# The first cross-attention of a Perceiver block: another order of key copies, scores, output projection and weighing

## The reference, cut to what matters

```python
def _L0_xattn_ref(query, key, value, mask, Wq, bq, Wk, bk, Wv, bv, Wo, bo):   # 16 heads of 16
    q = _split_heads(query @ Wq + bq)
    k = _split_heads(key @ Wk + bk)
    v = _split_heads(value @ Wv + bv)
    scores = jnp.einsum('bhqd,bhkd->bhqk', q, k) / jnp.sqrt(jnp.asarray(HS, q.dtype))
    scores = scores + mask * -1000000000.0
    attn = jax.nn.softmax(scores, axis=-1)
    out = jnp.einsum('bhqk,bhkd->bhqd', attn, v)
    out = out.transpose(0, 2, 1, 3).reshape(query.shape[0], query.shape[1], -1)
    return out @ Wo + bo
x = x + _L0_xattn_ref(_layernorm(x, axis=-1), ctx_1024, ctx_1024, mask, ...)
x = x + _L0_attn_ref(...)       # self-attention with compressed keys
x = x + _L0_ffn_ref(...)        # 8 experts, top 2
x = x + _L1_xattn_ref(...)      # the second cross-attention
x = x + _L1_attn_ref(...)
x = x + _L1_ffn_ref(...)
```

## Time and profile before

| what | value |
|---|---|
| median of 3 runs | 1205.26 us (1203.36 to 1205.91) |
| the profiled execution, its own time | 1215.15 us |
| its span in the trace | 1213.3 us |
| TensorE matmuls busy over the span | 946.6 us (78%) |
| VectorE busy | 581.1 us (48%) |
| ScalarE busy | 454.8 us (37%) |
| GpSimd busy | 338.9 us (28%) |
| first cross-attention, first scores to last addition to x | 26.2 to 252.0 us of the span |

### The profile page before, as it was taken

How to read it: one execution, slowest core, us unless ns; L and a number is a source line. 1 busy time by engine, 2 the same in 40 slices (tenths; PEclk the granted TensorE clock), 3 DMA queues, 4 the chain that set the end, 5 groups by cost and what they waited for, 6 DMA issues and landing times.

```text
span 1213.3 us, 24253 instructions
## 1 busy us (share of the span) xinstructions
PE 946.6 (78%) x8634; PEld 747.8 (62%) x8634; DVE 581.1 (48%) x1758; ACT 454.8 (37%) x1306; POOL 338.9 (28%) x502
## 2 busy tenths in 40 slices
PE   5899999979786399999814788888887663399980
PEld 3677777744664199999703556656555553399980
DVE  4556556530564201111276688788886563022222
ACT  3566666633222033333202465555555551011000
POOL 3211112001100500000262577666863241300004
PEclk9899999989797599999957799999998885699995
DMA  8111116000000678888310011111000001689953
GB/s 259 37 37 37 36 35 235 2 1 0 1 1 1 234 300 321 330 332 326 121 39 35 1 37 36 37 37 35 0 2 1 2 2 55 244 305 333 336 190 104
DMA packets 50562, 135.76 MB, mean 112 GB/s; under 512 B 16168, under 2 KB 37552, under 8 KB 44464
## 3 DMA queue, kind: packets, MB, share of 16 engines
q1 hardware_dynamic: 47408, 126.28, 29.1%
q0 software_dynamic: 3072, 8.39, 2.1%
HBM read 117.35 MB, written 17.30 MB: 111 GB/s over the span
## 4 chain that ended last, share of the span: by engine, by line
PE 59%; DVE 22%; issue 8%; POOL 3%; ACT 2%; SPq 2%; DMA 1%; another core or an unknown queue 1%; DVEq 0%; POOLq 0%; ACTq 0%
PE lower L998 14%; PE upper L1007 10%; PE upper L619 7%; PE upper L587 5%; PE upper L655 3%; PE lower L641 2%; PE upper L672 2%; PE upper L780 2%; PE upper L689 2%; DVE arena L1417 2%; DVE arena L1389 1%; DVE arena L1453 1%; POOL xslot L1941 1%; PE upper L957 1%; DVE x L1785 1%
## 5 line engine op out<-in xcount | busy, mean ns | idle before, releaser
L998 PEld LDWEIGHTS lower<-arena 128*128 128x128 f32 x1472 | 175.1, 195 | 6.1 <-DVE arena L1751 3.9
L998 PE MATMUL lower<-arena 128*128 128x128 f32 x1472 | 176.0, 279 | 2.6 <-DVE arena L1751 2.6
L619 PE MATMUL upper<-wkv,arena 128*128 128x256 f32 x512 | 141.3, 400 | 12.0 <-ACT arena L1098 6.8
L1007 PE MATMUL upper<-arena 128*128 128x256 f32 x552 | 126.4, 379 | 0.0
L1947 POOL DMA_INDIRECT arena<-yslot,slot x32 | 30.8, 962 | 323.4 <-DMA yslot<-arena 314.3
L619 PEld LDWEIGHTS upper<-wkv,arena 128*128 128x128 f32 x512 | 91.0, 193 | 34.8 <-issue 12.4
L1007 PEld LDWEIGHTS upper<-arena 128*128 128x128 f32 x552 | 101.5, 190 | 12.0
L1312 ACT ACTIVATE arena<-lower,arena 128x128 f32<-128x128 f32 x184 | 52.4, 370 | 106.4 <-PE lower L998 106.4
L1123 ACT ACTIVATE arena<-lower,arena 128x257 f32<-128x257 f32 x128 | 59.6, 475 | 61.0 <-DVE arena L1395 61.0
L1851 POOL TENSOR_TENSOR arena<-arena 128x512 f32<-128x512 f32 x64 | 70.6, 1114 | 36.1 <-ACT klast L1176 20.7
L655 PE MATMUL upper<-const,arena 128*128 128x128 f32 x512 | 78.0, 275 | 1.7 <-ACT arena L1133 1.4
(11 more groups left out here) (231 smaller groups left out, 1727.6 us busy)
## 6 DMA issues: line engine op xcount, KB each, us to landing
arena<-in_ew_dram SPq DMA_DIRECT2D x23, 2048.0 KB, 7.1
arena<-in_ew_dram SPq DMA_DIRECT2D x23, 1536.0 KB, 6.1
arena<-in_ctxT_dram SPq DMA_DIRECT2D x16, 1028.0 KB, 5.2
xslot<-zero SPq DMA_DIRECT2D x2, 2944.0 KB, 15.2
arena<-xslot SPq DMA_DIRECT2D x46, 128.0 KB, 5.8
yslot<-arena SPq DMA_DIRECT2D x46, 128.0 KB, 6.1
const<-in_const_dram SPq DMA_DIRECT2D x1, 1151.0 KB, 7.6
x<-in_x_dram SPq DMA_DIRECT2D x1, 1024.0 KB, 5.7
```

What stands on the lines that cost most here:

```text
L619: ins = mm(bank[6 + w][:, 0:D], dctx[k2][:, c, j2, w * P:w * P + P], wkv[l][:, c, D:2 * D], start=(c == 0), stop=(c == KC - 1))
L998: ins = mm(bank[1 + half][:, i * P:i * P + P], ew[k][:, at:at + P], exT[k % 2][:, c, :], start=(c == 0), stop=(c == KC - 1))
L1007: ins = mm(bank[4 + k % 2][:, 0:D], eh[k % 2][:, i, :], ew[k][:, at:at + D], start=(i == 0), stop=(i == nh - 1))
```

## The change

It gives the first cross-attention (`l` = 0) slot orders of its own on TensorE, ScalarE and VectorE. The second keeps the order it had. No instruction is added or taken away, and no function that a slot calls is changed.

- TensorE: scores, turns 0, keys 0, keys 1, values 0, project, turns 1, values 1, weigh.
- ScalarE: turned, keys 0, keys 1, exps 0, exps 1, values 0, values 1, shared.
- VectorE: maxima, shares, merge of batch b - 1, added, turned.
- GpSimd and SyncE are unchanged.

```diff
@@ TensorE
+                def first_slot(n, k, j, it):
+                    scores(n, k, j, it)
+                    turns(n, k, j, it, 0)
+                    keys(n, k, j, it, 0)
+                    keys(n, k, j, it, 1)
+                    values(n, k, j, it, 0)
+                    if there(n):
+                        project(n, k, j)
+                    turns(n, k, j, it, 1)
+                    values(n, k, j, it, 1)
+                    weigh(n, k, j, it)
+
                 def slot(n, k, j, it):
+                    if l == 0:
+                        first_slot(n, k, j, it)
+                        return
                     turns(n, k, j, it, 0)
                     scores(n, k, j, it)
@@ ScalarE
+                def first_slot(n, k, j, it):
+                    turned(n, k, j, it)
+                    keys(n, k, j, it, 0)
+                    keys(n, k, j, it, 1)
+                    exps(n, k, j, it, 0)
+                    exps(n, k, j, it, 1)
+                    values(n, k, j, it, 0)
+                    values(n, k, j, it, 1)
+                    shared(n, k, j, it)
+
                 def slot(n, k, j, it):
+                    if l == 0:
+                        first_slot(n, k, j, it)
+                        return
                     turned(n, k, j, it)
                     squares(n, k, j, it)
@@ VectorE
+                def first_slot(n, k, j, it):
+                    n0, k0, j0, _ = ahead(n, k, j, it, -1)
+                    maxima(n, k, j, it)
+                    shares(n, k, j, it)
+                    if there(n0):
+                        merge(n0, k0, j0)
+                    if j == 1 and there(n) and not (isinstance(n, int) and n == 0):
+                        added(n - 1)
+                    turned(n, k, j, it)
+
                 def slot(n, k, j, it):
+                    if l == 0:
+                        first_slot(n, k, j, it)
+                        return
                     n0, k0, j0, _ = ahead(n, k, j, it, -1)
                     if there(n0):
                         merge(n0, k0, j0)
```

## The result

The changed kernel takes 1214.45 us, the median of four runs (1208.82 to 1215.74; a fifth execution on record took 1218.91), against 1205.39 for the kernel before in the same comparison: 9.1 us slower. The ratio on record is 1.0079, with a 95% interval of 1.0041 to 1.0116. A second comparison gave 1.0068 (1.0042 to 1.0093). Both the forecast direction and the stated range (1200 to 1216) hold. The point (1209.6) lies 4.9 us low, and the median lies just outside what the prediction called its forecast's own range, 1205 to 1214.

The account below looks back on a forecast made before the run. TensorE's stream was taken to set the pace in the first cross-attention. Terms -1.1 + 0.7 + 6.6 - 0.6 - 1.3 = +4.3 us on 1205.26 gave 1209.6; own range 1205 to 1214, stated range 1200 to 1216.

Parts of the forecast that it names:

- Plain slots: 16 slots without projection or GpSimd's run: 0.07 us less than 6.15 each, -1.1 us together (bounds -4.0 and +3.2).
- Wait (b): In plain slots, weighing waits for VectorE's copy of the second transposes: 1.49 us against 1.40 of cover.
- Wait (a): In plain slots, first values wait for ScalarE's key copy to empty their bank; charged 0.10 us (bounds 0 and 0.3).
- Exponentials: On ScalarE, now behind both key copies: they end at 5.6 us, before the transposes due at 6.7, so stay covered.
- Projection slots: Seven slots whose projection waits for VectorE's later merge: 8.00 us against 7.83 in the loop, level outside; +0.7 us.
- GpSimd's run: Six slots where GpSimd's products hold VectorE's moved shares and merge: 8.30 us against 7.20, +6.6 us (bounds 0 and +9).
- Start: Before weighing 0: early key copies let batch 0's transposes start sooner, weighing 0 at 41.8 instead of 42.41, -0.6 us.
- End: From weighing 29 to weighing 31: 9.0 us instead of 10.31, -1.3 us (bounds -2 and 0).
- The signs named: Expected in the profile after: plain slots 6.0 to 6.15, projection waiting some 0.3, VectorE copy's waits on TensorE above 20.
- rival 1: Faster: small VectorE instructions fit between GpSimd's products and plain slots reach 5.90; -5.2 us, 1200.1; chance 0.2.
- rival 2: No measurable change: only the shares are held, 0.6 per run instead of 1.1; +1.3 us, 1206.6; chance 0.22.
- rival 3: Much slower: values wait 0.3 in every slot and the merge's last step is held; +11.9 us, 1217; chance 0.13.

Follow-up runs that it names:

- e1: Changed kernel with GpSimd's slot of the first cross-attention held until the merge of the batch before is done; 1193.73 us, ratio 0.9890 to the kernel before.
- e6: Changed kernel with ScalarE's exponentials between the two key copies again; 1216.99 us, one run.
- e4: Changed kernel with VectorE's shares and merge ahead of the maxima again; 1192.62 us, ratio 0.9872 to the kernel before.
- e3: Changed kernel with the second value product computed three times in the six slots with GpSimd's run; 1208.34 us, ratio 1.0021 to the kernel before.
- e9: Changed kernel unaltered, measured once more; 1214.16 us, ratio 1.0068 to the kernel before.
- e8: Changed kernel with TensorE's output projection directly behind the scores again; 1242.67 us, one run.
- e7: Changed kernel with TensorE's weighing ahead of the second value product again; 1251.65 us, one run.
- e2: Kernel before, with GpSimd's slot of the first cross-attention held until the next batch's maxima are done; 1194.99 us, ratio 0.9905 to the kernel before.
- e5: Changed kernel with e4's order on VectorE and e2's wait on GpSimd; 1186.00 us, ratio 0.9852 to the kernel before.

## Why the prediction was right, and where it was short

- **Plain slots** (-1.1 forecast, -2.4 measured). The account of narrow and wide groups held (5.90 forecast without waits, 5.91 as 5.99 less the visible 0.08). Wait (b) is there, at 0.08 for the 0.09 worked out. Wait (a), charged with 0.10, costs 0.02: in e1's and the changed kernel's slots values start 1.74 behind keys, where two groups take 1.72.
- **Exponentials** were covered as said. e6 shows that from weighing 0 on they are so with the copies in the old order, too.
- **Projection slots** (+0.7 forecast, +0.2 measured). The serial chain stands in the trace; in the loop 7.92 for the 8.00 worked out. The projection comes 4.10 behind the scores for 4.16, the copy 2.20 later as said. Outside the loop these slots took 7.51 in the kernel before, not the 7.56 that the prediction found as a remainder (a slot of 6.43, with 0.21 of waiting, and small differences were in it), and 7.45 after: I had booked no gain, and there was 0.06 in each.
- **GpSimd's run** (+6.6 forecast, +6.7 measured). Step by step in the loop: shares due at 4.3, ended 5.3 (5.25 forecast), merge's second step ended 6.3 (6.4), copy at 6.6 (6.66), weighing at 7.4 (7.50). The slots take 8.22 in the loop for 8.30, and 7.96, 8.39 and 8.70 outside it, where 8.30 had been put too; that the sum agrees to 0.1 is in part luck. e1 and e4 show from both sides that this meeting is the cause: either GpSimd or VectorE moved out of the way brings the slots to 6.0 to 6.1. The rule of the Trainium skill on the shared pair of ports ("SBUF — State Buffer", "Who interferes with whom") says as much, also that an instruction with one input outside SBUF isn't held; L1453's 0.28 agrees.
- **What failed** is a term that the sum lacks. Under "Slots with GpSimd's run" I priced the stand of TensorE at its own length and let the next slot be a plain one; that a stand of 2.1 to 2.6 us costs TensorE its clock, and 1.6 us more, in about half of the cases, was not in it. The kernel before stands 1.0 us at most between 60 and 235 us and its clock stays at 1.00. Measured: +4.8 us in the profile, about the 4.9 by which the point was low; the other terms missed by -1.3 (plain), -0.5 (projection), +0.1 (run), +1.2 (start) and +0.6 (last projection), which cancel to 0.1. That the range held in spite of the missing term is luck: nothing in it was put there for such a loss. Rows of the start had shown the pace halved after a stand, and I used it there alone. The Trainium skill, "TensorE: Matmul & The Clock Gate", section "HAM oscillation — how this bites in real kernels", tells of such losses behind waits for a DMA of some 3 to 5 us. e3 agrees that the wait is the cause; as to its length, here waits for VectorE of 2.0 to 2.6 us were followed by the loss in 9 of 18 cases (changed, e6, e9), and the measurement decides.
- **Start** (-0.6 forecast, +0.6 measured, but -0.8 in e9 and -1.15 in e3 and e4, whose code up to there is the same but for VectorE's order in e4; +0.4 in e8). The mechanism is there and shown by e6, and its size lies within what one execution differs from another. The transposes came at 35.97 instead of 36.75, though the exponentials began 0.46 later (33.84 for 33.38); the rest depends on how soon the clock rises again: here the two key groups behind them still took 3.63 instead of 1.90.
- **End**: -1.3, as worked out (5.34 and 3.67 for 5.4 and 3.6). The last projection behind it is no part of it; it took 0.6 longer by its clock in this execution.
- **The signs named.** Shares and the merge's second step took 1.01 and 0.74 for "near 0.9", the projection waits 0.23 for 0.3. Two failed: plain slots take 5.99, just under the 6.0 to 6.15, and the waits for the copy L1445 are 11 (12 before), not above 20, since the 0.08 of the plain slots doesn't stand as a wait in the trace.

The three rivals are out. Small instructions don't slip between the products (rival 1), both held ones are held (rival 2), and nothing waits 0.3 in every slot, nor is the merge's last step held (0.23; rival 3). The slower side had another mechanism. The prediction said that its range reached to both outer rivals; rival 3, at 1217, lay outside it.

## What to carry to other kernels

When an instruction moves in an engine's queue, look at what the *other* engines do at its new place: here two VectorE instructions of 0.2 to 0.3 us moved into GpSimd's run made its slots 1.1 us longer than before and 2.2 longer than they are without that meeting, and moving either party away took 18 to 21 us off the stretch (e1, e4). A stand of TensorE can cost more than its length: here those of 2.0 to 2.6 us cost another 1.6 us in half of the cases. Whether one has cost the clock shows in the duration of the groups behind it. And a change of several parts is worth splitting: here the change without the move of shares and merge gains 1.3%, that move more than undoes the gain, and ScalarE's new order gives nothing in the slots and 1.3 to 2.1 us at the start. TensorE's order and the move of the addition on VectorE were not tried apart.

## What the runs showed of the hardware that I had not expected

- Extra matmuls where TensorE stands can shorten the kernel: e3, -5.4 us in the stretch for 10 us of work more.
- The loss of clock behind a stand is not fixed: with the same code three slots of six lost it in one execution (changed), four in another (e9), two in e6; behind the stands of 2.9 to 3.3 us in e7 five of six, behind those of 3.4 us in e8 six of seven. At the end of the stage, where TensorE stands several times for 0.7 to 1.9 us, the last projection was slow in changed, e2, e5, e7 and e8 and not in the other six.
- GpSimd's products had cost the start of the kernel before more than any slot: with them held back, weighing 0 comes 5.3 us earlier (e2 against before).
